# Bodies of the first cores first in the program, Wg asked for ahead of Wk, list tables over two units

## Chip, cores and metric

One Trainium2 chip, 8 cores. Every core works on its own half of one sequence; four sequences have two cores each. The metric is the time of the slowest core in device microseconds; a run lists the span and the granted TensorE clock of each.

## What is computed

The input x is 4 x 4096 x 1024. After a LayerNorm, two things are added to x: a gated linear attention, and a mixture of four experts of which each token takes two. Cut to what matters:

```
xn = layernorm(x)
q, k, v = xn@Wq, xn@Wk, xn@Wv                 # 4 heads, 256 and 512 wide
g  = log_sigmoid(xn@Wgk1@Wgk2 + b) / 16
# per chunk: qg = q*exp(cumsum g)*scale, kd = k*exp(-cumsum g)
# o = tril(qg@kd^T)@v + qg@S ;  S = S*exp(g_last) + kg^T@v
attn = (rmsnorm(o) * silu(xn@Wg)) @ Wo
scores = xn@gate_W ; top2, softmax of the two
expert(e) = layernorm(relu(layernorm(xn@W1[e]))@W2[e])
out = x + attn + (xn + sum of the two experts by weight)
```

## The kernel before, in words

**Who does what.** A core takes 18 tiles of 128 tokens (`NT`), in five blocks of 4, 2, 4, 4 and 4 (`BASE`, `TILES`). The cores with even numbers, here called the first cores, have the first rows of their sequence, the odd ones the last. The state S of the attention at the point where an odd core begins is not passed between cores: the odd core works it out for itself in `earlier`, from the keys and values of the rows before. The first core starts with a zero state and does block 0 instead, in `first_block`. Behind that point both run the same program, except that the first cores have four tiles more in the output product (`wo_run`) and eight more slots of 128 tokens in the experts.

**Bodies that only some cores run.** The program is the same for all cores, and a value in memory (`flag`, 1 on odd cores) says which body is run. `load_flag` reads it into a register of an engine. `branch(body1, body0)` writes both bodies into the instruction stream of each engine, the one for flag 1 inside `If`, the other inside `Else`, and brings the semaphores that fall short to equal counts with `sem_inc` at the end of the body. `last_branch` does the same for the last slots. Every engine works through its own stream in the order in which it was written.

**The start.** SP asks for the first four tiles. POOL asks, in this order, for five small constants (`d_c0`), for Wk in two halves (`s_wk`), and for fourteen loads that all count on one semaphore `d_c1`: the mask `c_mask`, the row `c_rst`, the tables for the lists, the gate's weights, and zeros into `list_d`, `xn_d` and `out_d`. `k_c1` means all fourteen. Then come the flag and the big `branch(earlier, first_block)`. In `first_block` POOL asks for Wg in quarters (`load_wg`), then for Wq and Wv. The four tiles are transposed (`f_T`), `m_gk1(0)` and `gates(0)` make the gate factors of unit 0, and `block_G(0)` makes the Silu of xn@Wg for the whole block: 16 groups of eight matmuls, each in one of the three banks of `rot`, each followed by a Silu on ScalarE that frees the bank. In `gates`, ScalarE takes exp and log, VectorE two running sums whose first operand is `c_rst` and which wait for `k_c1`, and ScalarE then takes three exponentials.

**Units.** A unit is one head of one block: Q, K, gates of the next unit, V, and beside them the attention of the unit before (`unit`). `unit` merges a hand-made list of side work into its groups: the first two items among Q and K, the rest among the V groups. In the last block (units 16 to 19) the side work of unit 17 is `lists`, a generator in four pieces, which works out on VectorE where each token goes in the experts' lists; its two small matmuls use a bank of `rot` as well. `scatter` then writes 36 columns to `list_d`, one at each step of a merge. Unit 16 also has the loads of Wo on POOL.

**The end.** `wo_run` multiplies by Wo, tile by tile. Then come the slots of the experts in a pipeline of `step(s, n)`: the last three of the common part and all behind them stand in `last_branch` as `rest(NS1)` (31 slots, odd cores) and `rest_all` (39 slots, first cores). `rest` begins by reading the slot registers again, which `drop_all` gave back.

Of the kernel before, what the change touches and what calls it, by code (L numbers as in the profile page):

```python
# [15 lines left out]
H = 4  # L16
HDV = DV // H
# [38 lines left out]
class Prog:  # L56
# [19 lines left out]
    def branch(self, body1, body0):  # L76

        begin = {s: s.n for s in self.owner}
        at = {eng: len(self.q[eng]) for eng in self.ENGINES}  # L80
        ways = []
        for body in (body1, body0):
            for s in self.owner:
                s.n = begin.get(s, 0)
            body()
            part = {}
            for eng in self.ENGINES:
                part[eng] = self.q[eng][at[eng]:]
                del self.q[eng][at[eng]:]
            ways.append((part, {s: s.n for s in self.owner}))  # L90
        end = {s: max(w[1].get(s, begin.get(s, 0)) for w in ways) for s in self.owner}
        for s, n in end.items():
            s.n = n
        for eng in self.ENGINES:
            fill = []
            for part, n in ways:
                fill.append([(s, n.get(s, begin.get(s, 0)), v) for s, v in end.items()
                             if self.owner[s] == eng and n.get(s, begin.get(s, 0)) < v])
                assert eng != "gpsimd" or not fill[-1]

            def one(e, part, fill):
                for f in part:
                    f(e)
                for s, n, v in fill:
                    if n > 0:
                        e.wait_ge(s.h, n)
                    e.sem_inc(s.h, v - n)  # L107

            def run(e, eng=eng, fill=fill):
                with e.If(self.vals[eng]["flag"] > 0):  # L110
                    one(e, ways[0][0][eng], fill[0])
                with e.Else():
                    one(e, ways[1][0][eng], fill[1])
            if ways[0][0][eng] or ways[1][0][eng] or fill[0] or fill[1]:
                self.q[eng].append(run)

# [54 lines left out]
    def last_branch(self, body1, body0):  # L171

        begin = {s: s.n for s in self.owner}
        at = {eng: len(self.q[eng]) for eng in self.ENGINES}
        ways = []
        for body in (body1, body0):
            for s in self.owner:
                s.n = begin.get(s, 0)
            body()  # L180
            ways.append({eng: self.q[eng][at[eng]:] for eng in self.ENGINES})
            for eng in self.ENGINES:
                del self.q[eng][at[eng]:]
        for eng in self.ENGINES:
            def run(e, eng=eng):
                self.drop_all(eng, e)
                with e.If(self.vals[eng]["flag"] > 0):
                    for f in ways[0][eng]:
                        f(e)
                    self.drop_all(eng, e)  # L190
                with e.Else():
                    for f in ways[1][eng]:
                        f(e)
            self.q[eng].append(run)

# [40 lines left out]
def build():  # L236
# [264 lines left out]
        gdma(dst, src, d_c0)  # L501
    k_c0 = (d_c0, d_c0.n)
    k_wk = None
    for hf in range(2):
        k_wk = gdma(s_wk[:, :, hf * 512:(hf + 1) * 512], rows(Wk[:, hf * 512:(hf + 1) * 512]),
                    d_wk)
# [7 lines left out]
                     (xn_d[T:T + 128, :], zpad), (out_d[T:T + 128, :], zpad)):  # L514
        gdma(dst, src, d_c1)
    k_c1 = (d_c1, d_c1.n)
    P.load_flag(nc, flag, ("sync", "gpsimd"))
    k_wv = [None] * H

    def load_wv(h, wait=()):  # L520
        k_wv[h] = gdma(s_wv[:, h, :, :], rows(Wv[:, h * HDV:(h + 1) * HDV]), d_wv[h], wait=wait)

    d_wg = [mksem(f"d_wg{i}") for i in range(H)]
    k_wg = [None] * H

    def load_wg(wait):
        for h in range(H):
            k_wg[h] = gdma(s_wg[:, :, h * HDV:(h + 1) * HDV],
                           rows(Wg[:, h * HDV:(h + 1) * HDV]), d_wg[h],
                           wait=wait if h == 0 else [])  # L530

    d_wq = mksem("d_wq")
    k_wq = [None]
# [689 lines left out]
    def lists():  # L1223
# [14 lines left out]
        for e_ in range(NE):  # L1238
            ts = V(lambda e, e_=e_: e.tensor_tensor_scan(
                out=r_f[:, :, e_], data0=c_one5[:, :].broadcast_to([128, NT]),  # L1240
                data1=tot[:, :, e_], initial=0.0, op0=ALU.mult, op1=ALU.add), wait=[t])

        t = V(lambda e: e.tensor_scalar(out=r_t[:, 0, :], in0=r_f[:, NT - 1, :], scalar1=127.0,
                                        scalar2=None, op0=ALU.add), wait=[ts])
# [12 lines left out]
        for e_ in range(1, NE):  # L1257
            a = V(lambda e, e_=e_: e.tensor_scalar(
                out=r_sf[:, 2, :], in0=c_slot[:, :], scalar1=r_t[:, 3, e_:e_ + 1], scalar2=None,
                op0=ALU.is_ge), wait=[kb, k_c1] + xtm_free + ([prev] if prev else []))  # L1260
            step = float((e_off[e_] - e_off[e_ - 1]) // 2)
            if e_ == 1:
                b_ = V(lambda e: e.tensor_copy(out=r_sf[:, 0, :], in_=r_sf[:, 2, :]), wait=[a])
                prev = V(lambda e, step=step: e.tensor_scalar(
                    out=r_sf[:, 1, :], in0=r_sf[:, 2, :], scalar1=step,
                    scalar2=float(e_off[0] // 2), op0=ALU.mult, op1=ALU.add), wait=[a])
            else:
                b_ = V(lambda e: e.tensor_tensor(out=r_sf[:, 0, :], in0=r_sf[:, 0, :],
                                                 in1=r_sf[:, 2, :], op=ALU.add), wait=[a, prev])
                prev = V(lambda e, step=step: e.scalar_tensor_tensor(  # L1270
                    out=r_sf[:, 1, :], in0=r_sf[:, 2, :], scalar=step, in1=r_sf[:, 1, :],
                    op0=ALU.mult, op1=ALU.add), wait=[a, b_])
        V(lambda e: e.tensor_copy(out=r_sl[:, 0:2, :], in_=r_sf[:, 0:2, :]), wait=[prev])
        V(lambda e: e.tensor_scalar(out=r_sl[:, 2, :], in0=r_sf[:, 1, :], scalar1=512.0,
                                    scalar2=None, op0=ALU.add))
# [178 lines left out]
    def block_units(b):  # L1454
# [6 lines left out]
        for h in range(H):  # L1461
            u = 4 * b + h
            side = []
            if b + 1 < NB:
# [3 lines left out]
                elif h == 1 and TILES[b + 1] == 4:  # L1468
                    side = [lambda: m_LN(t0 + 2), lambda: (m_LN(t0 + 3), m_put(t0 + 2),
                                                           m_put(t0 + 3))]  # L1470
                elif h == 2:
                    side = [lambda: m_route(b + 1)]
                elif h == 3:
                    side = [lambda: m_gk1(b + 1)]
            elif h == 1:
                pieces = lists()
                side = [lambda: next(pieces)] * 4
            elif h == 2:
                side = [lambda: load_ogl(1), lambda: scale_wo(0), lambda: scale_wo(1)]
            elif h == 3:  # L1480
# [41 lines left out]
    def first_block():  # L1522
# [4 lines left out]
        xnT_free.clear()  # L1527
        for a in (nm_tok, xst_tok, xm_tok, xnT_tok, gk1_tok, Eq_tok, Em_tok, eb_tok, rt_tok):
            a.clear()
        load_wg([])  # L1530
        f_put()
        for tc in range(4):
            f_T(tc)
# [338 lines left out]
def make_inputs(core, inp):  # L1872
# [27 lines left out]
    if hh:  # L1900
# [6 lines left out]
                                     dtype=np.float32),  # L1907
        "xf_tm": np.ascontiguousarray(x[b, hh * (T - 512):hh * (T - 512) + 512, :],
                                      dtype=np.float32),
        "flag": np.full((1, 1), hh, np.int32),  # L1910
        "xp_tm": np.ascontiguousarray(x[b, 0:T, :], dtype=np.float32),
        "Wq": f32("L0_attn_Wq"), "Wk": f32("L0_attn_Wk"), "Wv": f32("L0_attn_Wv"),
        "Wg": f32("L0_attn_Wg"), "Wgk1": _pk(f32("L0_attn_Wgk1")),
# [35 lines left out]
```

How the kernel before makes its waits and increments, by code:

```python
            def one(e, part, fill):  # L101
                for f in part:
                    f(e)
                for s, n, v in fill:
                    if n > 0:
                        e.wait_ge(s.h, n)
                    e.sem_inc(s.h, v - n)
# [12 lines left out]
            def run(e, toks=tuple(toks)):  # L120
                for s, v in toks:
                    e.wait_ge(s.h, v)
# [10 lines left out]
        def run(e, fn=fn, wait=wait, inc=inc, inck=inck):  # L133
            for s, v in wait:
                e.wait_ge(s.h, v)
            r = fn(e)
            if inc is not None:
                r.then_inc(inc.h, inck)
# [8 lines left out]
        def run(e):  # L147
            for s, v in wait:
                e.wait_ge(s.h, v)
            self.drop(eng, e, (key[0], key[1] - (3 if eng == "tensor" else 4)) + key[2:])
            self.vals[eng][key] = nc.values_load(
                ap, engines=(et,), min_val=0, max_val=top,
                skip_runtime_bounds_check_because="computed from counts of at most 2048")
# [57 lines left out]
        def run(e):  # L211
            with e.If(self.vals[eng][key] > least - 1):
                e.wait_ge(tok[0].h, tok[1])
```

## Time and profile before

| | us |
|---|---|
| median of 3 runs | 1209.06 (1207.42 to 1212.25) |
| the profiled execution | 1210.35 |
| its span, core 0 (the slowest) | 1208.2 |
| spans of cores 0, 2, 4, 6 | 1208.2, 1207.8, 1205.1, 1207.3 |
| spans of cores 1, 3, 5, 7 | 1181.5, 1188.6, 1193.4, 1191.2 |
| core 0: TensorE, VectorE, ScalarE, GpSimd busy | 1005.1, 613.4, 538.9, 226.0 |

PE is TensorE, DVE VectorE, ACT ScalarE, POOL GpSimd, SP the queue engine. A row of a timeline gives start, length, engine, line, operation, output and input, the number of instructions merged, and in brackets the idle time before it with what ended it; "issue" there means that the profile shows nothing that it waited for. A busy share over the whole span says little here, since the stages have different limits; the timelines of the stages are what is read.

### The profile page before, as it was taken

The page shows a single profiled execution, that of the slowest core. Times are in us where ns is not written, and L with a number is a line of the kernel's source. Part 1 is how long each engine was busy: PE and PEld are TensorE (multiplying, and loading weights), DVE is VectorE, ACT ScalarE, POOL GpSimd, SP SyncE. Part 2 cuts the span into 40 slices and gives each one's busy share as a digit, 9 for nine tenths or more (in the row PEclk, how much of TensorE's full clock was granted, in tenths as well). Part 3 has the DMA queues.
Part 4 walks back from the last instruction along what each step waited for, and adds up shares of the span by engine and source line. Part 5 has one row for each costly group of instructions (what it writes and reads, how often), then busy time and mean ns, then how long its engine had stood idle before and what let it go on. Part 6 is the DMA issues. An engine that isn't in the chain of part 4 may idle for free.

```text
span 1208.2 us, 21526 instructions; the slowest of 8 cores (1181.5 to 1208.2 us)
## 1 busy us (share of the span) xinstructions
PE 1005.1 (83%) x4822; PEld 437.6 (36%) x4822; DVE 613.4 (51%) x1259; ACT 538.9 (45%) x1128; POOL 226.0 (19%) x271
## 2 busy tenths in 40 slices
PE   1588896889788988899688989897589999969983
PEld 1243333434333433344233334342234444424431
DVE  2224763643476347643676411125266766646772
ACT  3335443543554435343332211206276676747772
POOL 6000000000000000001033370104134332312321
PEclk9799997899999989999989999998799999989996
DMA  9996132430333152228237999869799977755744
GB/s 212 165 199 116 45 79 62 95 80 15 100 79 84 31 119 50 61 53 140 53 79 191 264 319 237 228 169 148 131 142 186 157 121 127 130 104 97 127 76 70
DMA packets 164301, 149.26 MB, mean 124 GB/s; under 512 B 119580, under 2 KB 131916, under 8 KB 164144
## 3 DMA queue, kind: packets, MB, share of 16 engines
q0 software_dynamic: 40624, 84.55, 37.7%
q1 hardware_dynamic: 120960, 53.76, 21.4%
q10 hardware_dynamic: 2592, 9.44, 2.5%
q8 instruction: 60, 0.98, 0.3%
q14 instruction: 65, 0.53, 0.2%
HBM read 111.58 MB, written 44.93 MB: 130 GB/s over the span
## 4 chain that ended last, share of the span: by engine, by line
PE 54%; DMA 14%; ACT 9%; issue 9%; DVE 9%; POOL 1%; SPq 1%; DVEq 1%; ACTq 0%; POOLq 0%
PE pb L453 36%; PE pb L1647 16%; DMA s_xr<-x_tm 5%; DMA s_xgT<-s_xg 3%; DMA s_wg<-Wg 3%; ACT s_hT L1731 2%; DMA s_kdT<-s_kd 1%; DMA out<-s_xr 1%; DVE s_L L982 1%; ACT s_z L1755 1%; PE pb L458 1%; DVE s_W L1107 1%; SPq L467 1%; PE pb L1669 1%; ACT s_sq L1113 1%
## 5 line engine op out<-in xcount | busy, mean ns | idle before, releaser
L1647 PE MATMUL pb<-s_we,s_xgT 128*128 x624 | 149.1, 394 | 39.8 <-DMA s_xgT<-s_xg 21.1
L453 PE MATMUL pb<-s_wv,s_xnT 128*128 128x512 bf16 x576 | 146.3, 402 | 23.6 <-ACT s_v L1057 12.1
L1647 PE MATMUL pb<-s_we,s_hT 128*128 x624 | 148.7, 381 | 0.0
L453 PE MATMUL pb<-s_wo,s_ogl 128*128 128x512 bf16 x576 | 133.5, 386 | 12.4 <-DMA s_ogl<-og_d 3.9
L453 PE MATMUL pb<-s_wg,s_xnT 128*128 128x512 bf16 x576 | 129.5, 383 | 10.6 <-DMA s_wg<-Wg 10.3
L1107 DVE SCALAR_TENSOR_TENSOR s_W<-s_W,s_eb,pb 128x512 bf16<-128x512 bf16 x144 | 100.9, 742 | 45.1 <-PE pb L453 44.6
L1731 ACT ACTIVATE s_hT<-pb,s_gbs 128x128 bf16<-128x128 bf16 x312 | 116.7, 459 | 4.6 <-PE pb L458 4.6
L1767 POOL DMA_INDIRECT out<-s_y,s_list x39 | 61.7, 1583 | 256.3 <-DVE s_rf L1692 170.8
L1647 PEld LDWEIGHTS pb<-s_we,s_xgT 128*128 128x128 bf16 x624 | 62.1, 101 | 118.6 <-issue 60.2
L1755 ACT ACTIVATE s_z<-pb,s_rf 128x512 bf16<-128x512 f32 x78 | 56.5, 774 | 102.0 <-DVE s_rf L1692 102.0
L453 PEld LDWEIGHTS pb<-s_wv,s_xnT 128*128 128x128 bf16 x576 | 55.7, 102 | 105.0 <-issue 53.2
L1113 ACT ACTIVATE s_sq<-pb 128x512 bf16<-128x512 f32 x72 | 42.9, 596 | 104.0 <-PE pb L453 83.8
L453 PE MATMUL pb<-s_xnT,s_wk 128*128 128x512 bf16 (+1 forms) x320 | 69.8, 371 | 18.6 <-DVE s_qg L1017 18.6
L1405 DVE TENSOR_TENSOR s_xr<-s_xr,pb 128x512 f32<-128x512 f32 x36 | 24.6, 687 | 119.0 <-PE pb L453 82.2
L453 PEld LDWEIGHTS pb<-s_wg,s_xnT 128*128 128x128 bf16 x576 | 56.3, 99 | 79.1 <-issue 14.6
L453 PEld LDWEIGHTS pb<-s_wo,s_ogl 128*128 128x128 bf16 x576 | 54.4, 99 | 79.7 <-issue 20.7
L1647 PEld LDWEIGHTS pb<-s_we,s_hT 128*128 128x128 bf16 x624 | 56.5, 98 | 64.9 <-issue 10.2
L1658 DVE TENSOR_TENSOR s_z<-pb,s_b 128x512 bf16<-128x512 f32 x78 | 51.6, 688 | 49.2 <-PE pb L1647 38.5
L1001 ACT ACTIVATE s_silu<-pb 128x512 bf16<-128x512 f32 x72 | 42.5, 597 | 75.6 <-PE pb L453 75.6
L453 PE MATMUL pb<-s_xnT,s_wq 128*128 128x512 bf16 (+1 forms) x320 | 67.9, 367 | 5.4 <-DVEq L107 4.8
L1389 ACT ACTIVATE s_xr<-s_xr,s_rs 128x1024 f32<-128x1024 f32 x18 | 22.3, 1239 | 101.8 <-DMA s_xr<-x_tm 101.8
L453 PE MATMUL pb<-s_W,s_qg 128*128 128x512 bf16 x144 | 47.5, 389 | 21.2 <-DVE s_W L1107 20.3
(182 smaller groups left out, 1283.1 us busy)
## 6 DMA issues: line engine op xcount, KB each, us to landing
s_we<-W POOLq DMA_DIRECT2D x64, 256.0 KB, 15.6
s_xr<-x_tm ACTq DMA_DIRECT2D x18, 512.0 KB, 7.9
out<-s_xr SPq DMA_DIRECT2D x18, 512.0 KB, 7.8
s_ogl<-og_d SPq DMA_DIRECT2D x16, 512.0 KB, 10.4
s_x<-x_tm POOLq DMA_DIRECT2D x12, 512.0 KB, 5.7
og_d<-s_ogT POOLq DMA_DIRECT2D x12, 512.0 KB, 3.0
s_wg<-Wg POOLq DMA_DIRECT2D x4, 1024.0 KB, 38.8
s_wv<-Wv POOLq DMA_DIRECT2D x4, 1024.0 KB, 66.4
```

Source lines behind the costliest of these rows:

```text
L453: lambda e: e.matmul(out=out, lhsT=lhsT, rhs=rhs, start=start, stop=stop),
L458: lambda e: e.transpose(out=out, in_=in_, identity=c_id[:, :]),
L1001: k = A(lambda e: e.activation(out=s_silu[:, i, h * HDV:(h + 1) * HDV], in_=bk[bi], func=ACT.Silu), wait=[t] + ([silu_free[(h, i)]] if (h, ...
L1107: W_tok[kc] = V(lambda e, pi=pi, kc=kc: e.scalar_tensor_tensor(out=s_W[:, kc, :], in0=s_W[:, kc, :], scalar=s_eb[:, kc, BASE[b] + c:BASE[b ...
L1113: ka = A(lambda e: e.activation(out=s_sq[:, :], in_=bk[oi], func=ACT.Square, accum_out=s_ssq[:, par, 0, c:c + 1]), wait=[to] + sq_tok[0] + ...
L1389: tb_tok[q] = A(lambda e: e.activation(out=s_xr[q % 4][:, :], in_=s_xr[q % 4][:, :], func=ACT.Identity, scale=s_rs[:, 2, n:n + 1], bias=s_ ...
L1405: k = V(lambda e: e.tensor_tensor(out=xs, in0=xs, in1=bk[bi], op=ALU.add), wait=[t, tb_tok[q]])
L1647: t = P.emit("tensor", lambda e, dc=dc: e.matmul(out=ps, lhsT=lhs[:, dc, :], rhs=P.window("tensor", e, ("w", s, hf), s_we[layer][dc], 512) ...
L1658: k = V(lambda e: e.tensor_tensor(out=zt[:, hf * 512:(hf + 1) * 512], in0=bk[bi], in1=P.window("vector", e, ("v", s), s_b1, 512, hf * 512) ...
L1731: k = A(lambda e, dc=dc: e.activation(out=s_hT[p][:, dc, :], in_=bkh[bi][:, dc * 128:(dc + 1) * 128], func=ACT.Relu, scale=s_gbs[:, s % 3, ...
L1755: S[s]["n2"] = A(lambda e, hf=hf, bi=bi: e.activation(out=s_z2[p][:, hf * 512:(hf + 1) * 512], in_=bk[bi], func=ACT.Identity, scale=s_rf[: ...
L1767: S[s]["put"] = P.emit("gpsimd", lambda e: e.indirect_dma_start(out=out_d, out_offset=bass.IndirectOffsetOnAxis(ap=s_list[:, s, 0:1], axis=0),
```

## The change

The two bodies of `branch` and of `last_branch` change places in the program: what was in `Else` is now in `If`. The flag is 1 on the first cores now, so each core still runs its own body. POOL reads the flag after the five small constants, and in a branch of its own the first cores ask there for the four quarters of Wg, ahead of Wk and of the fourteen loads; in `first_block` the request is gone and the counts are set as if it had been made there. `lists` is cut into six pieces rather than four, and they are the side work of units 16 and 17, three each.

```diff
@@ branch
                 with e.If(self.vals[eng]["flag"] > 0):
+                    one(e, ways[1][0][eng], fill[1])
+                with e.Else():
                     one(e, ways[0][0][eng], fill[0])
-                with e.Else():
-                    one(e, ways[1][0][eng], fill[1])
@@ last_branch
                 with e.If(self.vals[eng]["flag"] > 0):
-                    for f in ways[0][eng]:
+                    for f in ways[1][eng]:
                         f(e)
                     self.drop_all(eng, e)
                 with e.Else():
-                    for f in ways[1][eng]:
+                    for f in ways[0][eng]:
                         f(e)
@@ build, behind the five small constants
+    P.load_flag(nc, flag, ("gpsimd",))
+    k_wg = [None] * H
+    d_wg = [mksem(f"d_wg{h}") for h in range(H)]
+
+    def load_wg(wait):
+        for h in range(H):
+            k_wg[h] = gdma(s_wg[:, :, h * HDV:(h + 1) * HDV],
+                           rows(Wg[:, h * HDV:(h + 1) * HDV]), d_wg[h],
+                           wait=wait if h == 0 else [])
+
+    def wg_first():
+        load_wg([])
+        for q in d_wg:
+            q.n = 0
+
+
+    P.branch(lambda: None, wg_first)
     for hf in range(2):
         k_wk = gdma(s_wk[:, :, hf * 512:(hf + 1) * 512], rows(Wk[:, hf * 512:(hf + 1) * 512]),
@@ build, behind the fourteen loads
-    P.load_flag(nc, flag, ("sync", "gpsimd"))
+    P.load_flag(nc, flag, ("sync",))
@@ lists, behind the four running sums, and behind the loop over experts
+        yield
@@ block_units
+            elif h == 0:
+                pieces = lists()
+                side = [lambda: next(pieces)] * 3
             elif h == 1:
-                pieces = lists()
-                side = [lambda: next(pieces)] * 4
+                side = [lambda: next(pieces)] * 3
@@ first_block
-        load_wg([])
+        for q in d_wg:
+            q.n = 16
         f_put()
@@ make_inputs
-        "flag": np.full((1, 1), hh, np.int32),
+        "flag": np.full((1, 1), 1 - hh, np.int32),
```

## Rows read from the trace of the kernel before

**Rows 1.** Spans and mean granted clock of the cores, from the table of all cores.

```profile
core 0: 1208.2 us, clock 0.945
...
core 5: 1193.4 us, clock 0.934
```

**Rows 2.** Timeline of core 0: start, length, engine, line, operation, count, idle before and releaser.

```profile
39.89 2.34 DVE L982 TENSOR_TENSOR_SCAN s_L<-c_rst,s_L 128x512 f32<-128x512 bf16 x2 [3.65 <-DMA out<-zpad]
...
44.32 0.20 ACT L991 ACTIVATE s_eb<-s_L 128x8 f32<-128x8 f32 x1
...
47.29 3.84 PE L453 MATMUL pb<-s_wg,s_xnT 128*128 128x512 bf16 x9 [10.30 <-DMA s_wg<-Wg]
...
50.94 1.28 ACT L1001 ACT_TABLE_LOAD   x1 [6.42 <-PE pb L453]
...
56.19 0.60 ACT L1001 ACTIVATE s_silu<-pb 128x512 bf16<-128x512 f32 x1 [1.13 <-PE pb L453]
...
76.65 0.95 PE L453 MATMUL pb<-s_gateW,s_xnT 128*128 128x4 bf16 x32
```

**Rows 3.** Core 0, views of s_wk, out (0 to 50 us) and s_wg: issue starts, issue to landing.

```profile
L462 POOL DMA_DIRECT2D s_wk<-Wk x2: 911/918/926, 4.5 to 5.4; - x2
...
DMA to landing us min/median/max: 15.0/18.7/22.3
...
L462 POOL DMA_DIRECT2D out<-zpad x1: 590/590/590, 13.2 to 13.2; - x1
...
DMA to landing us min/median/max: 26.6/26.6/26.6
...
L462 POOL DMA_DIRECT2D s_wg<-Wg x4: 903/913/928, 16.2 to 18.8; - x4
...
DMA to landing us min/median/max: 30.6/38.8/47.3
```

**Rows 4.** Busy time by windows, core 0: engines, PEclk, DMA share, GB/s at the end.

```profile
35.00:40.00 5.00, 0.61 (x2) 0.18 (x2) 1.35 (x3) 2.41 (x3) 0.00 (x0) 0.72 0.83 87
40.00:50.00 10.00, 2.71 (x7) 1.02 (x8) 2.23 (x2) 2.20 (x3) 0.00 (x0) 0.50 1.18 162
```

**Rows 5.** Timeline of core 0 at its entry into first_block.

```profile
25.27 1.28 ACT L1516 ACT_TABLE_LOAD   x1 [3.69 <-issue]
...
25.47 0.69 DVE L1518 COPY s_xnT<-pb 128x1024 bf16<-128x1024 bf16 x1 [5.74 <-issue]
```

**Rows 6.** TensorE at the last branch: core 0, then core 1 (timelines).

```profile
1079.46 6.37 PE L1647 MATMUL pb<-s_we,s_xgT 128*128 x16 [9.19 <-issue]
...
1120.86 5.05 PE L1647 MATMUL pb<-s_we,s_xgT 128*128 x16 [2.40 <-ACT s_hT L1731]
```

**Rows 7.** The meeting of the two bodies: core 1, then core 0 (timelines).

```profile
275.96 1.91 PE L453 MATMUL pb<-s_xnT,s_wq 128*128 128x256 bf16 x16 [1.26 <-ACT s_silu L1001]
...
198.20 0.42 DVE L1017 TENSOR_TENSOR s_qg<-pb,s_Eq 128x256 bf16<-128x256 f32 x1 [2.89 <-PE pb L453]
```

**Rows 8.** Timeline of core 0 in units 16 to 18.

```profile
559.12 2.34 DVE L982 TENSOR_TENSOR_SCAN s_L<-c_rst,s_L 128x512 f32<-128x512 bf16 x2 [2.09 <-ACT s_L L979]
...
564.75 1.89 PE L453 MATMUL pb<-s_wv,s_xnT 128*128 128x512 bf16 x8 [1.92 <-ACT s_v L1057]
...
589.87 0.19 DVE L1225 CAST r_selb<-s_sel 128x72 bf16<-128x72 f32 x1
...
592.21 0.17 DVE L1243 TENSOR_SCALAR r_t<-r_f 128x4 f32<-128x4 f32 x1
...
597.67 0.20 DVE L1273 CAST r_sl<-r_sf 128x78 int32<-128x78 f32 x1
...
598.05 0.23 DVE L1283 TENSOR_TENSOR r_f<-r_f,s_gs 128x72 f32<-128x72 f32 x1
...
604.44 0.18 DVE L1319 COPY r_pair<-c_tok 128x18 int32<-128x18 int32 x1
...
605.83 3.57 PE L453 MATMUL pb<-s_xnT,s_wk 128*128 128x512 bf16 x8 [7.46 <-DVE s_qg L1017]
```

More of the change, by code:

```diff
@@ L521, in load_wv @@
         k_wv[h] = gdma(s_wv[:, h, :, :], rows(Wv[:, h * HDV:(h + 1) * HDV]), d_wv[h], wait=wait)
[L523 to L530, printed above, removed]
     d_wq = mksem("d_wq")
@@ L1272, in lists @@
                     op0=ALU.mult, op1=ALU.add), wait=[a, b_])
+        yield
         V(lambda e: e.tensor_copy(out=r_sl[:, 0:2, :], in_=r_sf[:, 0:2, :]), wait=[prev])
```

## Prediction, made before the change was run

> **What bounds the kernel now.** The table of cores is read first: the cores with the first rows of a sequence (even numbers) end last, core 0 at 1208.2 us, while the best placed of the others, core 5, ends at 1193.4 [rows 1]. So only what the first cores lose or win counts, until the others overtake them, and the others have 15 us of room. Next, the chain of waits and the timeline of core 0 from 0 to 80 us. TensorE does almost nothing until 47.29 us, and then it waits for the gate weights [rows 2]. Last, the timelines at the list code and at the last branch, which show two more idle stretches of TensorE (below).
>
> Sums are made against the profiled execution: 1210.35 us, of which the span of core 0 is 1208.2 and 2.15 lies around it. The median of the runs is 1209.06, 1.3 below, and I take 1.3 off at the end. A difference under 0.5% (6 us) could not be told from no change by a measurement like this.
>
> **Part 1: Wg ahead of Wk and of the constants.** POOL's loads land in the order in which they were issued: Wk's halves at 4.5 + 15.0 = 19.5 and 5.4 + 22.3 = 27.7, the last of the fourteen loads counted by `d_c1` (zeros into `out`) at 13.2 + 26.6 = 39.8, Wg's quarters from 16.2 + 30.6 = 46.8 to 18.8 + 47.3 = 66.1 [rows 3]. The DMA share is 0.83 even in its weakest stretch there [rows 4]: the queue is never without work, so its order decides who lands when. The four quarters of Wg take 66.1 - 39.8 = 26.3 us.
>
> After the change the order is small constants, Wg, Wk, `d_c1`, Wq, Wv. Wg's first quarter then takes Wk's old place and lands near 20, and its wait (10.3 us of idle TensorE [rows 2]) goes. What is late next? `gates(0)` is written ahead of `block_G(0)`, and its two scans wait for `k_c1`, all fourteen loads. In the trace the scan starts at 39.89, 0.1 us after the last of them landed [rows 2], and is named as waiting for it. Behind that scan in ScalarE's own order stand the three exponentials of gates(0), and behind those every Silu of block_G(0); behind the Silus stand the banks: `rot` has three, so TensorE can do three groups of Wg and then stops until the first Silu. The move puts the four Wg quarters and nothing less in front of the constants. The set of bytes up to there is the same as before up to Wg's last quarter, so the constants land near 66.1 (lower bound 62, if the flag's read on POOL and the early start give everything; upper bound 68.5, if the small descriptors run worse with nothing beside them).
>
> From there by core 0's rows: scan start to the end of the last exponential 44.52 - 39.89 = 4.63, a table load 1.28, the first Silu 0.60, about 0.2 of handing over: the fourth group can start 6.8 us after the constants, at 72.9. Thirteen groups are left. The granted clock will be at its lower level, 1.2 GHz, after 30 us of idling; it was 0.50 of full speed from 40 to 50 us, with TensorE idle [rows 4], and at 47.29 nine matmuls took 3.84 us: some 3.5 for a group of eight. The rest go at the pace of the Silus, 0.60 and 1.13 of waiting for TensorE, 1.73 us [rows 2]: 12 x 1.73 = 20.7. End: 72.9 + 3.5 + 20.7 = 97.1. Before, the groups ended where the gate scores begin, 76.65 [rows 2]. **Cost: 20.4 us** (16 to 23 with the bounds). I see nothing behind it that takes it back: Q, K, V follow without waiting for their weights, and Wq and Wv keep their places in the queue.
>
> Rule of the Trainium skill against this reading: DMA: Bandwidth & Descriptors, "Queues, rings and completion order", says that completion is not FIFO per issuing engine, that each of the 16 engines has its own ring, and that a small DMA can use fewer of them. By that, small constants could overtake. The trace agrees only so far: the rule leaves the order within one ring, and a load with Wg in front of it in each ring stays behind it; the landings here are in order of issue.
>
> **Part 2: the first cores' bodies stand first.** Entering the far body of `If` costs something: on core 0 ScalarE sat 3.69 and VectorE 5.74 us with nothing that the profile shows, at the first instruction of `first_block` [rows 5]. That goes for these cores, but the time in front of the scan is then only slack before the constants: gain nothing. It would cost if the cover went, and that is the case of rival B.
>
> The last branch is different. On core 0 TensorE idles 9.19 us, and 16 matmuls then take 6.37 instead of 3.61 (the clock has fallen). On core 1, which enters its body directly, the same place costs 2.40 of idling and 5.05 for the matmuls [rows 6]. Difference: (9.19 + 6.37) - (2.40 + 5.05) = 8.1. **Gain: 8.1 us** for the first cores (5 to 10), all on the path, since the slots behind it follow TensorE.
>
> The same 8.1 us go to the others' account, and up to 3.7 at their start, where ScalarE's copy comes right behind its norms; the skipped part of `wo_run` may cost them another jump (0 to 9). Core 5: 1193.4 + 8.1 + 2.5 - 2.8 (part 3) = 1201.2, up to 1210: still under the first cores.
>
> At the end of `first_block` these cores now leap over `earlier`. The others leap there today: TensorE's wait on core 1 is 1.26 us in all, and names ScalarE [rows 7]. On core 0 VectorE has 2.89 us before its first product is due [rows 7], and its leap is covered up to that; a leap as long as the 5.74 above would show 2.9. **Cost: 1 us** (0 to 4).
>
> **Part 3: list code over two units.** Today VectorE does it in one stretch, 589.87 to 604.62, and TensorE idles 7.46 us for `s_qg`; its next eight matmuls take 3.57 instead of 1.89, 1.7 more, and with the products behind them I put the slow stretch at 2.3 [rows 8]. The new pieces: counts and scans (2.2 us) after Q of unit 16, slot tables (5.4, to 597.57) after K of unit 16, the rest of the tables (0.5) after V; 2.7 + 3.8 = 6.5 us remain at the end of unit 17, which end at about 596.4, before the second product of unit 18 is needed. So the 7.46 + 2.3 = 9.8 go.
>
> But the 5.4 us now stand ahead of the scans of `gates(17)` on VectorE (559.12 today), behind which ScalarE has Eq, Em, eb and the copies `s_v`, for which TensorE waits already (1.92) [rows 8]. Counts: TensorE's two products wait for VectorE's cast, an estimated 1.7 us. Last K product then at 558.7, tables to 564.1, scan at 564.1 rather than 559.12: 5.0 us later, and TensorE's wait grows from 1.9 to 5 us or more, long enough for the clock to fall (2.0 more). Cost 7.0. **Net gain 2.8 us** (from 8 gain, if ScalarE's part finds cover, to 4 loss).
>
> **Sum.** 1210.35 + 20.4 - 8.1 + 1.0 - 2.8 = 1220.9; less 1.3: 1219.6 us.
>
> **Rivals.**
>
> A, the forecast: 1219.6. For it: the scan's named wait and the landing order.
>
> B, the constants do not queue behind Wg (they land at 40 as before). The fourth group then starts at 46.7, ends 24.2 later at 70.9, 5.8 earlier than now: 1210.35 - 5.8 + 1 - 2.8 - 8.1 = 1194.7 for the first cores, and now the others set the time: 1201.2 to 1210, plus 2.15 less 1.3: about 1206. Against it: fourteen loads in order of issue. The point from which it decides: with constants before 55.5 the first cores no longer lose in sum.
>
> C, the last branch's wait is reloading of slot registers and not the leap, so that standing first changes nothing there: 1219.6 + 8.1 = 1227.7. Against it: core 1 reloads the same registers in 2.40 us.
>
> D, list tables and the join cost their upper bounds: 1219.6 + 6.8 + 3 = 1229.4.
>
> **How the numbers follow.** A 0.66, B with its in-between values (constants at 45 to 58) 0.16, C 0.08, D 0.10. The range holds A with part 1's bounds and half of the others' (1211 to 1228) and reaches to the middle of B: 1206 to 1229. Faster by over 0.5% (under 1203): 0.06, the lower end of B. Within 0.5%: 0.18, most of B and the lowest of A. Slower: 0.76.
>
> **What would show it.** On core 0 after: Wg's first quarter landed by 22; three groups of s_wg and then a gap of about 30 us; the scan L982 at about 66 named as waiting for `out<-zpad`; gate scores at about 97. The last branch with a wait of 2 to 3 us instead of 9.2. No wait of 7.46 at unit 18, but one of about 5 at `s_v` of unit 16. The prediction is wrong if the scan starts before 55, or if the 20 us found at 97 are not there at 800.

## The result, and the profile after

The changed kernel takes 1221.26 us (median of its runs; 1211.37 for the kernel before, timed beside it): a ratio of 1.0087 [1.0054, 1.012]. It is slower, by some 10.5 us, and the forecast was 1219.6. Times are medians of all executions; the ratios, and the means over several executions below, leave out those in which the cores of a die showed a lower granted clock and took longer (one of five here).

The table of cores in the profiled execution after (span, then the mean granted clock) shows first cores that end 6 to 13 us later than in [rows 1] and its table, and odd cores that are 7.5 us later on the mean, all of them still before the first cores:

```profile
core 0: 1214.2 us, clock 0.939
core 1: 1200.4 us, clock 0.929
core 2: 1218.2 us, clock 0.939
core 3: 1186.5 us, clock 0.933
core 4: 1217.8 us, clock 0.944
core 5: 1196.7 us, clock 0.929
core 6: 1214.6 us, clock 0.944
core 7: 1201.0 us, clock 0.927
```

**The start.** The timeline of core 0 after, which answers to [rows 2] (start, length, engine, line, operation, output and input, count, idle before and releaser):

```profile
9.00 3.54 POOL L462 DMA_DIRECT2D s_wg<-Wg  x4 [4.44 <-issue]
...
31.36 7.03 PE L453 MATMUL pb<-s_wg,s_xnT 128*128 128x512 bf16 x24 [0.31 <-issue]
...
66.45 2.34 DVE L990 TENSOR_TENSOR_SCAN s_L<-c_rst,s_L 128x512 f32<-128x512 bf16 x2 [36.16 <-DMA out<-zpad]
...
68.89 1.15 ACT L993 ACTIVATE s_Eq<-s_L,c_cv 128x1024 bf16<-128x1024 f32 x1 [35.48 <-DVE s_L L990]
...
71.11 1.28 ACT L1009 ACT_TABLE_LOAD   x1
...
73.67 25.50 PE L453 MATMUL pb<-s_wg,s_xnT 128*128 128x512 bf16 x104 [35.29 <-ACT s_silu L1009]
99.01 0.95 PE L453 MATMUL pb<-s_gateW,s_xnT 128*128 128x4 bf16 x32
```

Read it from the bottom up. TensorE does 24 products of Wg (three groups of eight, one for each bank), and then sits for 35.29 us; what released it is the first Silu. ScalarE had waited 35.48 us for VectorE's scan, and VectorE 36.16 us for a DMA before that scan. The name of that DMA is `out<-zpad`, the last of the fourteen loads. The landings on core 0, which answer to [rows 3] (Wk, `c_rst`, `out`, Wg):

```profile
L462 POOL DMA_DIRECT2D s_wk<-Wk x2: 923/928/933, 12.5 to 13.4; - x2
DMA to landing us min/median/max: 39.2/42.2/45.1
...
L462 POOL DMA_DIRECT2D c_rst<-resetb x1: 637/637/637, 14.2 to 14.2; - x1
DMA to landing us min/median/max: 43.6/43.6/43.6
...
L462 POOL DMA_DIRECT2D out<-zpad x1: 617/617/617, 21.1 to 21.1; - x1
DMA to landing us min/median/max: 45.3/45.3/45.3
...
L462 POOL DMA_DIRECT2D s_wg<-Wg x4: 896/907/913, 9.0 to 11.6; - x4
DMA to landing us min/median/max: 10.5/22.7/33.2
```

So Wg is complete at 11.6 + 33.2 = 44.8 where it was at 66.1, and `out` lands at 21.1 + 45.3 = 66.4 where it was at 39.8. The row `c_rst`, all that the scan reads of the fourteen, was there at 14.2 + 43.6 = 57.8. The busy times by windows (engines, granted clock, DMA share, GB/s) show that the queue was full all the while, TensorE doing nothing at a granted clock of 0.54:

```profile
40.00:66.00 26.00, 0.00 (x0) 0.00 (x0) 0.00 (x0) 0.00 (x0) 0.00 (x0) 0.54 1.09 161
```

**The lists** (core 0 after, against [rows 8]; then the first K products of unit 18):

```profile
589.38 0.20 DVE L1279 SCALAR_TENSOR_TENSOR r_sf<-r_sf 128x39 f32<-128x39 f32 x1
589.55 2.34 DVE L990 TENSOR_TENSOR_SCAN s_L<-c_rst,s_L 128x512 f32<-128x512 bf16 x2
...
595.18 3.46 PE L453 MATMUL pb<-s_wv,s_xnT 128*128 128x512 bf16 x8 [5.20 <-ACT s_v L1065]
...
628.39 3.62 PE L453 MATMUL pb<-s_xnT,s_wk 128*128 128x512 bf16 x16
```

The scan of the gates starts the moment that the slot tables end, TensorE's wait for `s_v` has grown from 1.92 to 5.20 us, and eight products behind it take 3.46 rather than 1.89; in return the wait of 7.46 us at unit 18 is gone. **The last branch** (core 0, then core 5) is the mirror image of [rows 6]:

```profile
1087.80 3.61 PE L1660 MATMUL pb<-s_we,s_xgT 128*128 x16 [2.22 <-ACT s_hT L1744]
...
1134.35 6.22 PE L1660 MATMUL pb<-s_we,s_xgT 128*128 x16 [10.07 <-issue]
```

**One core is not enough.** Core 0 ends only 6.0 us later, though it was 22 us behind in the middle. Single cores scatter by some us in the expert slots, so the four first cores are taken together. Means of cores 0, 2, 4, 6 in the profiled execution, from the rows of each core: the start of the gate scores, of the first product by Wo, of the first slot, of the first product of the last branch, and the span. The kernels below those two are the experiments of the next section.

| kernel | gate scores | Wo | first slot | last branch | span |
|---|---|---|---|---|---|
| before | 77.8 | 650.9 | 810.8 | 1077.7 | 1207.1 |
| after | 99.6 | 672.0 | 833.1 | 1089.0 | 1216.2 |
| Wg alone | 98.3 | 672.4 | 837.3 | 1097.2 | 1225.8 |
| both branches alone | 76.1 | 652.9 | 812.0 | 1069.8 | 1197.9 |
| lists alone | 78.0 | 650.5 | 810.7 | 1074.5 | 1204.3 |
| after less Wg's move | 78.0 | 650.1 | 809.8 | 1066.1 | 1193.4 |
| after, own semaphore for c_rst | 91.0 | 662.4 | 823.5 | 1079.8 | 1207.6 |
| after, c_rst first | 66.7 | 651.6 | 812.3 | 1069.1 | 1197.1 |

The first two lines give the story: +21.8 at the gate scores, +21.1 at Wo, +22.3 at the first slot, then +11.3 at the last branch, where the leap is gone, and +9.1 at the end. Each line is one execution, and differences of 2 or 3 us between two lines can be scatter: the kernel of the last experiment below (the flag's read alone) is 3.5 later at Wo than before and no slower. Where it matters, the first cores' spans are therefore also given as a mean over all executions: 1215.6 after, and 1204.5, 1204.9 and 1206.2 before, in the three sessions in which the experiments were run.

### The profile page after: what moved, and what is told of

It reads as the page before. It is cut to its first block, busy times and chain, and to the rows that moved or that the text cites. A ratio compares the mean times of both kernels' runs of the same rounds, so it can differ in the third digit from the quotient of the medians.

```text
span 1218.2 us, 21450 instructions; the slowest of 8 cores (1186.5 to 1218.2 us)
## 1 busy us (share of the span) xinstructions
PE 996.5 (82%) x4729; PEld 437.1 (36%) x4822; DVE 613.8 (50%) x1259; ACT 538.1 (44%) x1128; POOL 225.9 (19%) x271
## 4 chain that ended last, share of the span: by engine, by line
PE 53%; DMA 15%; ACT 10%; issue 9%; DVE 8%; DVEq 1%; SPq 1%; POOL 1%; ACTq 0%; POOLq 0%; another core or an unknown queue 0%
PE pb L453 35%; PE pb L1660 16%; DMA s_xr<-x_tm 6%; DMA out<-zpad 4%; ACT s_hT L1744 2%; DMA s_xgT<-s_xg 2%; DVE s_L L990 2%; DMA s_xg<-xn_d,s_list 1%; DMA out<-s_xr 1%; ACT s_z L1768 1%; PE pb L458 1%; PE pb L1682 1%; ACT s_sq L1121 1%; DVE s_W L1115 1%; SPq L467 1%
## 5 line engine op out<-in xcount | busy, mean ns | idle before, releaser
L1660 PE MATMUL pb<-s_we,s_xgT 128*128 x608 | 144.1, 389 | 28.3 <-DMA s_xgT<-s_xg 14.8
L1660 PE MATMUL pb<-s_we,s_hT 128*128 x609 | 144.5, 380 | 2.5 <-issue 1.4
L453 PEld LDWEIGHTS pb<-s_wv,s_xnT 128*128 128x128 bf16 x576 | 56.3, 102 | 111.0 <-issue 59.6
L990 DVE TENSOR_TENSOR_SCAN s_L<-c_rst,s_L 128x512 f32<-128x512 bf16 (+1 forms) x40 | 42.5, 1105 | 73.8 <-ACT s_L L987 37.2
L1399 ACT ACTIVATE s_xr<-s_xr,s_rs 128x1024 f32<-128x1024 f32 x18 | 22.3, 1239 | 101.9 <-DMA s_xr<-x_tm 101.9
## 6 DMA issues: line engine op xcount, KB each, us to landing
s_ogl<-og_d SPq DMA_DIRECT2D x16, 512.0 KB, 10.3
s_wg<-Wg POOLq DMA_DIRECT2D x4, 1024.0 KB, 24.2
s_wv<-Wv POOLq DMA_DIRECT2D x4, 1024.0 KB, 66.1
```

Of the source, the lines that this page charges most:

```text
L453: lambda e: e.matmul(out=out, lhsT=lhsT, rhs=rhs, start=start, stop=stop),
L990: ts = V(lambda e, k=k: e.tensor_tensor_scan(out=s_L[:, k, 0:N], data0=c_rst[:, 0:N], data1=s_L[:, k, 0:N], initial=0.0, op0=ALU.mult, op1 ...
L1399: tb_tok[q] = A(lambda e: e.activation(out=s_xr[q % 4][:, :], in_=s_xr[q % 4][:, :], func=ACT.Identity, scale=s_rs[:, 2, n:n + 1], bias=s_ ...
L1660: t = P.emit("tensor", lambda e, dc=dc: e.matmul(out=ps, lhsT=lhs[:, dc, :], rhs=P.window("tensor", e, ("w", s, hf), s_we[layer][dc], 512) ...
```

## Experiments

Theory: the change is a sum of three parts that hardly touch each other, and only Wg's move loses. It loses since the scan of `gates(0)` stands in front of every Silu and waits for a semaphore that counts fourteen loads, which now land behind Wg. The rivals were that the loads need not queue, that the last branch's wait is something else than its place, and that the loss is given back later.

**Each part alone.** First Wg's move (`load_wg` in its own branch ahead of Wk, flag read there, all else as before):

```diff
+    P.load_flag(nc, flag, ("gpsimd",))
+    P.branch(lambda: None, wg_first)
...
-        load_wg([])
+        for q in d_wg:
+            q.n = 16
```

> The kernel before with the early request for Wg alone (bodies and list code as before). Theory: the fourteen loads of d_c1 stand behind Wg and Wk, so on core 0 the scan of gates(0) starts at 65 to 69 us and names out<-zpad, the gate scores start at 97 to 101 instead of 76.7, and the time is 1211 + 20 to 25 = 1231 to 1236. Rival, that the 22 us of the changed kernel come from the order of the bodies or from the late Wk: the scan starts at 40 to 45 and the time is 1205 to 1213.

Measured: 1236.15 us (1233.4 without two executions at a lower clock), ratio 1.0175 [1.0113, 1.0237]. VectorE, then TensorE at the last branch, core 0:

```profile
67.61 2.34 DVE L990 TENSOR_TENSOR_SCAN s_L<-c_rst,s_L 128x512 f32<-128x512 bf16 x2 [31.83 <-DMA out<-zpad]
...
1098.20 6.41 PE L1656 MATMUL pb<-s_we,s_xgT 128*128 x15 [8.84 <-issue]
```

The loss is whole, and so is the old wait at the last branch. Then the two branches turned round, without the rest:

```diff
                 with e.If(self.vals[eng]["flag"] > 0):
+                    one(e, ways[1][0][eng], fill[1])
...
-        "flag": np.full((1, 1), hh, np.int32),
+        "flag": np.full((1, 1), 1 - hh, np.int32),
```

> The kernel before with the two bodies exchanged alone. Theory: on the first cores TensorE's wait at the last branch falls from 9.2 to about 2.3 us and its matmuls behind it from 6.4 to 3.6 to 5; at the meeting of the bodies they lose 1 to 3 us; sum 1211 - 9 + 2 = 1204, with the odd cores 3 us later at their start and 8 to 9 later at the last branch, ending at 1195 to 1206. Rival, that the wait at the last branch is the reading of slot registers: wait stays at 9 us, time 1211 to 1214.

Measured: 1205.46 us, 0.9927 [0.9895, 0.996]. The end of it is an odd core now in the profiled execution: core 7 at 1205.1, while the first are at 1194.3 to 1200.6. And the lists alone (the two added `yield`, three pieces each in units 16 and 17):

> The kernel before with the list code over two units alone. Theory: the wait of 7.46 us for s_qg in unit 18 goes (with the slow matmuls behind it, 9.8), the wait for s_v in unit 16 grows from 1.92 to 5.2 and the products for the counts cost 1.3; net gain 3 to 3.5 us, time 1208. Rival, that the two waits cancel: 1211, and the start of the output product on core 0 at 649 to 650 as before instead of 646.

Measured: 1208.28 us, 0.9983 [0.9957, 1.0009]: by the time alone not to be told from nothing, and Wo on core 0 starts at 651.9, where the expectation had 646 for the gain and 649 to 650 for its rival. The start of Wo carries all the scatter of the stages before it, though. Counted from the last gate scores of the last block (491 us) to Wo, the first cores take 158.4 to 158.8 us before (mean 158.6), 155.3 on all four with the lists alone, and 155.2 on the mean in the changed kernel: the gain is there, 3.3 us. (In all the kernels here it is 158.3 to 160.9 without the lists' change and 155.1 to 157.9 with it.) The trace has both sides of the trade: no wait for `s_qg` at unit 18, and on core 0

```profile
575.43 3.43 PE L453 MATMUL pb<-s_wv,s_xnT 128*128 128x512 bf16 x8 [5.35 <-ACT s_v L1057]
```

Of 1211 us, the three are +21.2, -8.8 and -2.1; their sum is +10.3, where the whole change is +0.87%, 10.5. The parts add up within their intervals, which are some 7, 4 and 3 us to either side; that the two sums meet to 0.2 is luck. The first cores' spans over all executions give +21.0, -8.1 and -2.7.

**Where c_rst stands in the queue, and what it is counted with.** If the wait for the fourteen loads is the cause, the loss must follow the one small load that the scan needs. In both kernels it has a semaphore of its own, and all else is as in the changed kernel. In the first it stands in front of Wg. In the second it stands right behind Wk, which is where the changed kernel has it too, as the first of the fourteen: this run changes the semaphore alone. The edit of the first:

```diff
+    k_rst = gdma(c_rst[:, :], resetb, mksem("d_rst"))
...
-                op0=ALU.mult, op1=ALU.add), wait=[t, k_c1])
+                op0=ALU.mult, op1=ALU.add), wait=[t, k_rst])
```

> The changed kernel, with c_rst loaded ahead of Wg and on a semaphore of its own, for which the scans wait instead of for all fourteen. Theory: the scan on the first cores starts at 34 to 36 us, the Silus run from 41, and the next thing late is the gate scores' wait for the other thirteen loads at about 67: scores start at 67 to 70 instead of 99. The first cores gain about 30 us and end near 1187, so that the odd cores (1186 to 1201 in the changed kernel) set the time: 1199 to 1205. Rival, that Wg's move costs through something else (Wk, the branch on POOL): the scan is early but the time stays at 1215 to 1221.

> The changed kernel with one edit: the row c_rst has a semaphore of its own and is asked for right behind Wk, in front of the other thirteen loads; the scans of the gates wait for it alone. Theory (the scan is late by exactly what stands in front of c_rst in POOL's queue): Wk's second half lands at about 60, so the scan starts at 60 to 61 on the first cores rather than at 66.5 to 68.8, the gate scores stand at 92 to 93 rather than 99, and the time is 6 to 7 us below the changed kernel: 1214 to 1216. Together with c_rst ahead of Wg (scan at 33.75) and the change itself (66.5) this is the third point on one line. Rival (c_rst lands only with the whole group, or the first Silu waits for something else): scan or gate scores as in the changed kernel, time 1219 to 1222.

Measured: 1204.32 us, 0.9912 [0.9879, 0.9945], and 1211.88 us, 1.0007 [0.9982, 1.0033]. The scans of the two on core 0, and the issue and landing of `c_rst` in the second:

```profile
33.75 2.34 DVE L991 TENSOR_TENSOR_SCAN s_L<-c_rst,s_L 128x512 f32<-128x512 bf16 x2 [3.73 <-ACT s_L L988]
```

```profile
60.80 2.34 DVE L991 TENSOR_TENSOR_SCAN s_L<-c_rst,s_L 128x512 f32<-128x512 bf16 x2 [30.58 <-DMA c_rst<-resetb]
...
L462 POOL DMA_DIRECT2D c_rst<-resetb x1: 632/632/632, 14.5 to 14.5; - x1
DMA to landing us min/median/max: 46.1/46.1/46.1
```

14.5 + 46.1 = 60.6: the scan starts 0.2 us behind the landing. The load is of 128 KB and took 46.1 us with 6 MB of Wg and Wk in front of it, but 7.7 us where it stands in front of them. The Trainium skill (DMA: Bandwidth & Descriptors, "Queues, rings and completion order") says, of the queues of SP and ScalarE, that completion is not FIFO per issuing engine. In POOL's queue the traces show a little of it: before the change `c_rst` landed ahead of Wk's second half, behind which it stands, on all four first cores (by 1.1 to 5.6 us; 26.4 against 32.0 on core 2). It got past the end of one load, and never past the 6 MB. The scans start at 67.3 (changed kernel), 59.6 (own semaphore) and 34.1 (own semaphore and in front), the gate scores at 99.6, 91.0 and 66.7, means of the first cores: the rival that small loads need not queue has fallen. The semaphore alone is worth 7.7 us of the 33 at the scan, the place in the queue the rest. The second kernel's gain is larger than I expected: 9.7 us by the ratios, not 6 to 7.

But in the first kernel gate scores 33 us earlier than after the change became only 20 at Wo. TensorE on core 0:

```profile
40.96 24.29 PE L453 MATMUL pb<-s_wg,s_xnT 128*128 128x512 bf16 x102 [2.86 <-ACT s_silu L1010]
66.94 0.94 PE L453 MATMUL pb<-s_gateW,s_xnT 128*128 128x4 bf16 x32 [1.69 <-DMA out<-zpad]
79.45 5.10 PE L453 MATMUL pb<-s_xnT,s_wq 128*128 128x512 bf16 x15 [11.56 <-DMA s_wq<-Wq]
```

The next thing late is Wq. It landed at 76.5 (20.6 + 55.9) before the change, where Q began at 77.67, and lands at 78.5 here: the bytes ahead of it are the same ones. My expectation of 1187 for the first cores was 10 us too good for this reason. **So an early Wg could not have brought the first Q forward at all**, even with `c_rst` in time: with all of it ahead of Wq, the bytes of the queue and not their order set when Q has its weights.

**The last branch, and the big one.** In the first kernel only the bodies of `last_branch` change places, in the second only those of `branch`.

```diff
@@ last_branch
-                with e.If(self.vals[eng]["flag"] > 0):
-                    for f in ways[0][eng]:
+                with e.If(self.vals[eng]["flag"] < 1):
+                    for f in ways[1][eng]:
```

> The kernel before with one edit: in last_branch alone the first cores' slots stand first in the program; the big branch, its entry and the join are as they were. Theory (the 9.19 us of idling there is the leap to the far body, and the leap over the other body at the join costs the first cores some 3.5 us only where the big branch is turned round too): on core 0 the wait at the first slot of the last branch falls from 9.2 to 2 to 3 us, Q of block 1 stays at 196 (it was 198.2 with both branches turned round), the first cores end 8 to 9 us earlier, at about 1199; the odd cores pay 7 to 9 us at their last branch (10 us of idling instead of 2.5) and end at 1189 to 1203. Time 1201 to 1204, so 0.992 to 0.994 of before. Rival (the wait is the reloading of slot registers): 1209 to 1212. Rival (what both branches turned round gave came from the big branch): last branch unchanged, time 1209 or more.

> The kernel before with one edit: the bodies of the big branch alone change places; the last branch stays. Theory (entering its body directly gives the first cores nothing, since they wait for constants and Wg anyway; at the end they leap over the other body): Q of block 1 on core 0 behind a wait of 5.1 to 5.6 us rather than 4.8, 1 to 3 us later than before counted from the gate scores; the last branch idles 9 to 10.5 us on the first cores; their spans 1206 to 1210, time 0.999 to 1.003 of before. Together with the last branch alone (first cores 8.0 us earlier on the mean) this gives what both did (9.2). Rival (the entry is worth its 3.7 to 5.7 us): gate scores at 71 to 73, 0.995 to 0.997.

Measured: 0.9958 [0.9936, 0.9981] (expected 0.992 to 0.994), and 1.0004 [0.9991, 1.0017]. The last branch alone, core 0 and then core 3, which pays what core 0 no longer does:

```profile
1070.20 5.30 PE L1647 MATMUL pb<-s_we,s_xgT 128*128 x16 [2.92 <-ACT s_hT L1731]
...
1139.74 6.35 PE L1647 MATMUL pb<-s_we,s_xgT 128*128 x16 [8.30 <-issue]
```

Its first cores' spans are 1199.1 on the mean, 8.0 under before (7.1 over all executions), where the forecast said 8.1; the time falls by less (some 5 us): core 6 at 1203.0 ends last in the profiled execution, and the odd core 3 is there at 1201.3. With the big branch alone, TensorE on core 0 at the join and at the last branch:

```profile
195.81 3.56 PE L453 MATMUL pb<-s_xnT,s_wq 128*128 128x256 bf16 x16 [6.28 <-issue]
...
1074.78 6.12 PE L1647 MATMUL pb<-s_we,s_xgT 128*128 x15 [9.00 <-issue]
```

The last branch keeps its 9 us, so these belong to its own place. The wait at the join is 6.1 to 6.4 rather than 4.8 to 4.9. The gate scores are 2.3 us earlier (75.5 on the mean), which I had put at nothing, but a gain from the entry isn't shown: with the same bodies in the same order they stand at 76.1 (both branches) and 77.9 (both and the lists), and with the old order at 77.0 to 78.0. From the gate scores to the join's Q it is 123.1 us here and 120.5 to 122.9 in the other kernels with the new order in which Q follows the gate scores at once, and 119.5 (before) to 122.0 in five with the old one. So more than the wait itself says can't be put down to the join, and the span is 1206.6: nothing is left that can be told from zero. The Trainium skill (Runtime: NRT & Kernel Launch, "Instruction fetch mechanics") would have any taken branch out of the fetch window stall for the fetch; at the join, where the row of core 1 before showed nothing of it, TensorE of the first cores now waits 1.2 to 1.6 us longer.

**The change without Wg's move** (both branches and the lists), and the same with 0.75 MB of zeros for `xn_d` and `out_d` asked for behind the big branch:

```diff
-                     (xn_d[T:T + 128, :], zpad), (out_d[T:T + 128, :], zpad)):
+                     ):
...
     P.branch(earlier, first_block)
+    for dst, src in ((xn_d[T:T + 128, :], zpad), (out_d[T:T + 128, :], zpad)):
+        gdma(dst, src, d_c2)
```

> The changed kernel without its part 1: both branches turned round and the lists in six pieces over two units, but Wg asked for where it was before. Theory (the parts add up on the first cores, and Wg ahead of the constants is all that the change loses): first cores 3 us below the order alone (1194 to 1201), so 1191 to 1198; the odd cores, which reached 1205 with the order alone, get the lists' 3 us as well and set the time: 1201 to 1204, 17 to 20 us below the whole change. Rival (the lists' gain is gone where TensorE's pace is already set by the odd cores' other waits): 1205 to 1206. Rival (the parts do not add up): above 1207.

> Both branches turned round and the lists over two units, Wg where it was before (0.992 in the run above), and the two loads of zeros into xn_d and out_d asked for behind the big branch. Theory (until 78 us the first cores wait only for bytes that stand in POOL's one queue, and 0.75 MB of zeros cost some 7 us of it): Wg's quarters and Wq land 6 to 7 us earlier on core 0, the gate scores stand at 71 to 73 rather than 78.5, the first Q at 72 to 74 rather than 79.4, and Wo is asked for at 546 to 547 rather than 552.4; first cores 1186 to 1195, odd cores 1184 to 1194, time 1194 to 1198, so 0.986 to 0.990. Rival (as in the run with c_rst ahead of Wg, an earlier start is lost again behind 1060, where the last slots took 2.6 us longer): milestones as said, time 1198 to 1200.

Measured: 1199.28 us, 0.9919 [0.9893, 0.9945] (a little better than the 1201 to 1204 expected), and 1202.76 us, 0.9921 [0.9902, 0.9941]. The first is some 20 us under the whole change (0.9919 against 1.0087), which is the price of Wg's move once more, from the other side; its first and odd cores lie between 1186.9 and 1197.8. In the second the start behaves as expected: Wg is waited for until 41.58 and the gate scores stand at 70.6 rather than 78.5 on core 0, and Q follows at once:

```profile
41.58 18.79 PE L453 MATMUL pb<-s_wg,s_xnT 128*128 128x512 bf16 x78 [9.69 <-DMA s_wg<-Wg]
...
70.57 0.95 PE L453 MATMUL pb<-s_gateW,s_xnT 128*128 128x4 bf16 x32
71.80 3.40 PE L453 MATMUL pb<-s_xnT,s_wq 128*128 128x512 bf16 x15 [0.28 <-DVE s_gs L928]
```

But the 7 us are 3.2 at Wo (646.9 on the mean against 650.1), 1.3 in the first cores' span (1192.1 against 1193.4; 1.9 over all executions), and nothing in the time, where core 1 at 1196.9 stands beside core 2 at 1198.2. My expectation of 0.986 to 0.990 was missed, and its rival, that an earlier start is lost again, was right. The same edit on the kernel with `c_rst` first:

> The changed kernel with c_rst ahead of Wg under its own semaphore (1204.3, where Q of the first unit waited 11.56 us for Wq) and one edit more: the two loads of zeros into xn_d and out_d (0.75 MB in short pieces) are asked for behind the big branch. Theory (what the early gates won is lost again since Wq lands at 78.5 whatever TensorE does; it lands when the bytes in front of it are through): the eleven tables land at about 61, Wq at 72 to 73, Q begins at 73 instead of 79.45, and core 0 asks for Wo at about 546 instead of 551.8; first cores 1188 to 1195; the odd cores, 1187 to 1212 in that run, now set the time: 1200 to 1206. Rival (the zeros are cheap, being spread over all engines beside Wk): Wq at 77 to 79, core 0 at 551 as before, 1202 to 1206 too; so the landing of Wq and core 0's own milestones tell, not the time.

Measured: 1203.10 us, 0.9951 [0.993, 0.9972]. Gate scores at 64.3, Q behind a wait for Wq until 72.13 instead of 79.45, Wo at 646.8, spans of the first cores 1193.3, within 0.1 of those of the kernel whose gate scores stand at 78.0 (over all executions, 1194.9 and 1195.0). So a late start is handed on whole and an early one is not. Of what takes the early start back I can name Wq, which takes the first 7 of the 14 us. After it, the two kernels with early first Qs and the one with `c_rst` first take 157.4 to 157.7 us from the last block's gate scores to Wo, where the changed kernel takes 155.2; why, and what takes the rest behind Wo, stays open.

**The flag's read on POOL** is the one cost of part 1 that the forecast did not price by itself. The kernel before, with POOL's read moved in front of Wk:

> The kernel before with one edit: POOL reads the flag behind the five small constants, in front of Wk, and not behind the fourteen loads; no branch there, no load moved. Theory (the read idles POOL for 4.4 to 5.1 us with the transfers of SP running, but the queue catches up, since in the changed kernel the first load behind it landed at 20.4 where 19.5 was the landing before): Wk's first half asked for at 9 rather than 4.5, landed at 20 to 21; constants at 40 to 42; time within 2 us of before, 0.998 to 1.002. Rival (the 4.5 us are lost by all that is behind in the queue): constants at 44 to 45, gate scores on core 0 at 81 rather than 76.7, time 1214 to 1216, so 1.0035 to 1.004.

Measured: 1210.75 us, 1.0003 [0.9981, 1.0025]. Issue and landing on core 0, of Wk and of `out`:

```profile
L462 POOL DMA_DIRECT2D s_wk<-Wk x2: 896/904/911, 9.1 to 10.0; - x2
DMA to landing us min/median/max: 12.0/17.5/23.1
...
L462 POOL DMA_DIRECT2D out<-zpad x1: 577/577/577, 17.7 to 17.7; - x1
DMA to landing us min/median/max: 23.0/23.0/23.0
```

Asked for 4.6 us later, Wk's halves land at 21.1 and 33.1 rather than 19.5 and 27.7, but the last constant at 40.7 rather than 39.8: by then the queue has caught up. (That SP's transfers are through sooner in the meantime may be the reason; it was not tested.) Nobody waits for Wk there, and the time doesn't move.

## Why the prediction was right

**The mechanism.** The wait, the landing order and the path of part 1 are what the rows show, and each of the other parts is there in its own rows. One reading was too strong: the landings are not strictly in order of issue, since `c_rst` landed up to 5.6 us ahead of Wk's second half before the change. It didn't matter, because the scan waited for the last of the fourteen and nothing small got past Wg as a whole. And the page's sentence that the forecast weighed against itself is written for the queues of SP and ScalarE, so it was a weaker ground for B than it seemed.

**Part 1, 20.4 forecast, 21.2 measured** (Wg alone, interval 13.7 to 28.7; 20 by the difference to the change without it). Step by step on core 0: the constants forecast at 66.1, landed at 66.4; the scan forecast at about 66, started at 66.45; the fourth group at 72.9, started at 73.67; the gate scores at 97.1, came at 99.01. The scan was 0.35 later than forecast, the way from it to the fourth group 7.2 rather than 6.8, and from there to the scores 25.3 rather than 24.2. The last is the low clock, which lasted for one Silu more than I had put: its idle time is 2.34 rather than 1.13, and the granted clock was 0.50 from 73 to 77 us, 0.57 from 77 to 80 and 1.00 from 80 to 82 (ScalarE after, idle before each):

```profile
77.34 0.60 ACT L1009 ACTIVATE s_silu<-pb 128x512 bf16<-128x512 f32 x1 [3.37 <-PE pb L453]
80.28 0.60 ACT L1009 ACTIVATE s_silu<-pb 128x512 bf16<-128x512 f32 x1 [2.34 <-PE pb L453]
82.00 0.60 ACT L1009 ACTIVATE s_silu<-pb 128x512 bf16<-128x512 f32 x1 [1.13 <-PE pb L453]
```

"I see nothing behind it that takes it back" held up to the first slot (+22.3 on the mean of four). With Wg alone it is +20.5 at the gate scores, +21.5 at Wo, +26.5 at the first slot, +19.4 at the last branch and +18.7 at the end (+21.0 over all executions): handed on, with a scatter of some us.

**Part 2, -8.1 at the last branch, +1.0 at the join, so -7.1; -8.8 measured for both** (interval -12.7 to -4.8). On core 0 it was (9.19 + 6.37) - (2.22 + 3.61) = 9.7; the last branch alone gave 8.0 in the first cores' spans. At the join the row of TensorE on core 0 before, and those of TensorE and VectorE after, are

```profile
196.09 3.57 PE L453 MATMUL pb<-s_xnT,s_wq 128*128 128x256 bf16 x16 [4.81 <-DVEq L107]
...
221.41 3.57 PE L453 MATMUL pb<-s_xnT,s_wq 128*128 128x256 bf16 x16 [5.11 <-DVEq L107]
...
224.32 0.42 DVE L1025 TENSOR_TENSOR s_qg<-pb,s_Eq 128x256 bf16<-128x256 f32 x1 [3.70 <-issue]
```

where [rows 7] has 2.89 for VectorE, and TensorE waited 4.81 before: +0.8 and +0.3, of 1.0 forecast. In the kernels with the new order TensorE waits 5.1 to 6.4 there, so +0.3 to +1.6.

**Part 3, -2.8 forecast, -2.1 measured by the time** (-5.2 to +1.1), which alone shows nothing; the 3.3 us between the last gate scores and Wo show it, with the waits where the prediction had them: 7.46 gone, 1.92 grown to 5.20 (forecast 5), its eight products at 3.46 instead of 1.89.

**The others.** Core 5 was forecast at 1201.2 and ended at 1196.7; the four odd cores went up by 7.5 on the mean (1188.7 to 1196.2), of 7.8 forecast. They set nothing here, but they set the time as soon as the first cores are repaired: in the profiled execution of every kernel here under 1206 us an odd core is the slowest or within 4 us of it.

**The rivals.** B (constants land as before) fell with the 66.4. C (reloading of registers) fell with the last branch alone, where the registers are reloaded as before. D did not come. What was luck: by the separate runs part 1 cost 0.8 more than forecast, part 2 gave 1.7 more and part 3 gave 0.7 less, all inside intervals of several us, so a sum that comes within 2 us of the measured time owes some of that to chance. And a single core's span, 6.0 on core 0, would have called the sum wrong; the medians and the mean of four agree with it.

## What to carry to other kernels

When a load is moved to the front of a queue, ask of everything that it passes who waits for it, and through which semaphore: one semaphore over fourteen loads makes the first reader wait for the last of them (7.7 us here), and a small operand that stands at the head of a long chain deserves its own, early (the place was worth 25 more). Reordering this never empty queue moved the waits about; only bytes taken out of it brought the first Q forward, and little of that reached the end. And test an edit of several parts in parts: two of three here were gains, of some 9 and 2 to 3 us, hidden under one loss of 21. Where the time can't show a small part, a stretch between two milestones around it may: the lists' 3.3 us were the same on all four cores.

## What the runs showed that I had not expected

- A flag's read on POOL left 4.44 us of idle time in front of the next load (4.4 to 5.1 on all cores of the changed kernel). Behind the fourteen loads, as before, the read and the entry of the body left between nothing and 4.0 us on the first cores. What makes the difference was not tested. In the run with the read alone, the constants behind it landed only 0.9 us later.
- The place of a body costs 7.7 to 10.6 us of idle TensorE where it follows without a pause (last branch, both ways round, all kernels here; 2.1 to 3.5 where the body stands first), and 0.3 to 1.6 us more where TensorE waits for others anyway (the join). What the 8 to 10 us consist of was not separated.
- A delay at 70 us arrives at 1070 us nearly undiminished (+20.5 at the gate scores, +19.4 at the last branch, Wg alone), while 14 us of head start at the gate scores (78.0 to 64.3), 7 at the first Q, arrive as 2.6 at the last branch and as nothing at the end.
